# A two-layer decoder kernel: phase 2's work in a new order on all engines, and the second cross attention's scores computed as one unit

## The reference, cut to what matters

```
x = LN(x + self_attention_0(x))          16 heads, causal, with a bias      phase 1
x = LN(x + cross_attention_0(x, ctx))    16 heads, 64 keys, masked          phase 1
x = LN(x + moe_0(x))                     8 routed experts (top 2), 2 shared phase 2
x = LN(x + self_attention_1(x))          16 heads, causal, latent weights   phase 2
x = LN(x + cross_attention_1(x, ctx))    one head of 256 channels, 64 keys  phase 3
x = LN(x + ffn_1(x))                     1024 wide, sine activation         phase 3
```

```
qh = q @ Wq + bq;  kh = ctx @ Wk + bk;  vh = kh @ Wv + bv
scores = qh @ kh.T;  scores = where(mask == 0, -10000, scores)
out = softmax(scores) @ vh @ Wo + bo
```

## Time and profile before

| | value |
|---|---|
| median of 3 runs | 3624.59 us |
| profiled execution | 3628.03 us, span 3626.1 us |
| PE, PEld, DVE, ACT, POOL busy | 92%, 70%, 72%, 63%, 28% of the span |
| phase 1, with its prologue | from 0 to about 1305 us |
| phase 2 | to about 2987 us |
| phase 3 | to the end |
| mean granted TensorE clock | 0.969 of full |

### The profile page before, as it was taken

The page is one execution under the profiler, slowest core; times in us unless marked ns, Lnnn a source line. Parts: engine busy times, 40 slices in busy tenths (PEclk is TensorE's granted clock), DMA queues, the critical chain, the costliest instruction groups (busy, mean ns, idle before and its releaser), DMA issues.

```text
span 3626.1 us, 59862 instructions
## 1 busy us (share of the span) xinstructions
PE 3344.5 (92%) x20706; PEld 2528.1 (70%) x20706; DVE 2625.4 (72%) x7153; ACT 2283.5 (63%) x4067; POOL 1022.4 (28%) x1576
## 2 busy tenths in 40 slices
PE   5999999999999848999999999999999876999998
PEld 4677777777777636777777777777777655766664
DVE  5688888888888644677777777777777534788876
ACT  3677777777777622456666555556556543677776
POOL 2244444444444422222222322222223110000000
PEclk8999999999999979999999999999999877999999
DMA  7654545445544021444444444444444421011010
GB/s 193 101 95 84 88 96 107 84 88 95 107 84 82 17 82 53 84 80 77 86 92 94 94 88 88 90 89 93 92 87 88 73 44 62 12 36 35 25 35 24
DMA packets 203403, 283.27 MB, mean 78 GB/s; under 512 B 48929, under 2 KB 131874, under 8 KB 194274
## 3 DMA queue, kind: packets, MB, share of 16 engines
q1 hardware_dynamic: 203106, 279.46, 38.2%
HBM read 179.49 MB, written 96.73 MB: 76 GB/s over the span
## 4 chain that ended last, share of the span: by engine, by line
PE 71%; ACT 11%; DVE 7%; DMA 5%; issue 4%; SPq 1%; POOL 1%; PEld 0%; POOLq 0%; ACTq 0%; PEldq 0%; DVEq 0%
PE ps L829 35%; PE ps L1003 8%; PE ps L978 7%; PE ps L1201 5%; PE ps L1017 5%; ACT q_stack L1669 5%; PE ps L953 3%; DMA qk_scratch<-parts 3%; ACT pt L1686 2%; PE ps L984 1%; PE ps L1077 1%; PE ps L888 1%; PE ps L1028 1%; DMA k_stack<-qk_scratch 1%; DVE nmax L1351 1%
## 5 line engine op out<-in xcount | busy, mean ns | idle before, releaser
L1686 ACT ACTIVATE pt<-ps 128x512 f32<-128x512 f32 x1280 | 735.9, 598 | 346.7 <-PE ps L1003 338.8
L1889 POOL TENSOR_SCALAR_AFFINE_SELECT pt<-pt 128x256 f32<-128x256 f32 x1024 | 392.1, 419 | 704.9 <-ACT pt L1686 704.9
L978 PE MATMUL ps<-k_stack,q_stack 96*128 96x512 f32 (+3 forms) x2048 | 547.2, 338 | 42.3 <-ACT q_stack L1669 11.8
L1358 DVE CUSTOM_DVE_ANT_0 ps<-ps,future 128x512 f32<-128x512 f32 (+3 forms) x1024 | 481.7, 515 | 141.9 <-PE ps L978 138.8
L1003 PE MATMUL ps<-q_stack,k_stack 100*128 100x512 f32 (+3 forms) x2048 | 538.6, 345 | 29.3 <-ACT q_stack L1669 23.4
L1003 PEld LDWEIGHTS ps<-q_stack,k_stack 100*128 100x128 f32 x2048 | 351.5, 195 | 124.9 <-ACT q_stack L1669 37.2
L978 PEld LDWEIGHTS ps<-k_stack,q_stack 96*128 96x128 f32 x2048 | 355.6, 194 | 103.2 <-ACT q_stack L1669 18.8
L1351 DVE TENSOR_REDUCE nmax<-ps 128x1 f32<-128x512 f32 (+2 forms) x768 | 354.4, 502 | 92.0 <-PE ps L984 91.0
L1895 POOL TENSOR_TENSOR rs<-rs 128x4 f32<-128x4 f32 x96 | 97.1, 1012 | 1062.0 <-DVE rs L1394 1062.0
L1669 ACT ACTIVATE q_stack<-ps 4x512 fp32r<-4x512 f32 x512 | 300.8, 588 | 64.7 <-PE ps L992 56.5
L1017 PE MATMUL ps<-pt,v_ones 128*32 128x512 f32 (+3 forms) x4096 | 312.1, 446 | 5.7 <-POOL pt L1889 5.3
(11 more groups left out here) (278 smaller groups left out, 7958.6 us busy)
## 6 DMA issues: line engine op xcount, KB each, us to landing
qk_scratch<-parts SPq DMA_DIRECT2D x64, 1024.0 KB, 5.5
q_stack<-qk_scratch SPq DMA_DIRECT2D x384, 128.0 KB, 4.9
k_stack<-qk_scratch SPq DMA_DIRECT2D x384, 128.0 KB, 5.6
gate_of<-gate_scratch SPq DMA_DIRECT2D x128, 256.0 KB, 5.6
x_mid<-x_ring SPq DMA_DIRECT2D x32, 512.0 KB, 3.9
x_ring<-x_mid SPq DMA_DIRECT2D x32, 512.0 KB, 5.3
x_ring<-in_x SPq DMA_DIRECT2D x16, 512.0 KB, 3.8
out_dram<-x_ring SPq DMA_DIRECT2D x16, 512.0 KB, 2.9
```

Source lines behind the costliest of these rows:

```text
L978: done = e.matmul(bank(bank_of[piece])[:, at:at + width], a.q[0:96, base + h, t * P:(t + 1) * P], a.k[0:96, base + h, 0:width], start=a.la ...
L1358: done = e.tensor_tensor_reduce(src, src, future[:, SEQ - width:SEQ], -1.0, 3e38, ALU.add, ALU.min, nmax[:, g % 2, to:to + 1])
L1686: e.activation(dst, src, ACT.Exp).then_inc(exp_up.sem)
L1889: done = e.affine_select(out=blk, in_=blk, compare_op=ALU.is_ge, fill=0.0, base=0, pattern=[[0, 2], [1, P]], channel_multiplier=-1)
```

## The change

**Phase 2.** Every time of phase 2's table is new, on all five engines, and with it the order of the pieces and the choice of PSUM banks. No piece of phase 2 changes what it does. The table's period goes from 91.45 to 90.623. The table lines for some kinds:

```diff
-    2: (91.45, {
+    2: (90.623, {
+        "sync": {
+            "ld 2": [-78.284],
+            "send": [82.769, 104.563],
+            "rows": [112.457, 134.686, 155.546, 179.135],
+            "st 2": [279.788],
+            "gh": [-38.533],
+            "sg": [-36.173, -35.738, -26.135, -20.394, -5.291, 0.424, 9.165, 18.599],
+        },
...
         "scalar": {
-            "mr": [137.263, 139.255, 160.384, 164.751, 196.024, 196.044, 212.747, 212.767],
+            "mr": [138.106, 139.099, 158.603, 159.596, 191.074, 192.067, 210.72, 211.713],
...
         "vector": {
-            "h3": [-47.625, -31.127, -24.632, -21.3, -6.146, 7.033, 19.611, 23.072, 28.061, 40.153],
+            "h3": [-47.748, -31.792, -24.968, -18.789, -4.6, 5.128, 13.795, 20.052, 26.166, 33.951],
...
         "gpsimd": {
-            "sel": [144.512, 151.809, 165.914, 174.49, 195.45, 197.278, 214.007, 218.167],
-            "h2": [None, None, -34.818, -28.614, -14.445, -6.268, 1.14, 12.393, 18.268, 24.753],
+            "sel": [152.034, 156.648, 173.145, 180.159, 199.72, 203.91, 218.585, 226.305],
+            "h2": [None, None, -27.497, -21.756, -6.653, -2.324, 7.803, 17.237, 24.112, 31.773],
...
-        "sync": {
-            "ld 2": [-85.349],
-            "send": [76.442, 95.983],
-            "rows": [97.435, 117.928, 140.108, 160.952],
-            "st 2": [273.954],
-            "gh": [-46.706],
-            "sg": [-44.627, -44.367, -30.774, -27.299, -12.417, -5.729, 2.455, 17.582],
-        },
```

```diff
@@ phase 3's table, and pieces_of
         "gpsimd": {
+            "tb x1": [-26.6],
             "ln x1": [-4.648],
...
         put("tc", "x1", b)
+        put("tb", "x1", b)
@@ tensors
-        co_b, f2_b = sb(st3, "co_b_row", [1, DIM]), sb(st3, "f2_b_cols", [P, CT])
-        ones = sb(st3, "ones", [1, P])
+        co_b, f2_b = sb(st3, "co_b_rows", [P, DIM]), sb(st3, "f2_b_cols", [P, CT])
-        a_h, a_l = (sb(st3, f"a_{part}", [P, CT, keys_all], F32R) for part in "hl")
+        a_parts = sb(st3, "a_parts", [P, CT, BATCH, 2, CTX], F32R)
-        q_bias, seen, unseen = (sb(st3, n, [P, keys_all]) for n in ("q_bias", "seen", "unseen"))
+        seen, offset = (sb(st3, n, [P, keys_all]) for n in ("seen", "offset"))
-        LN_BIAS = {"x0": xo_b, "a1": proj_b}
+        LN_BIAS = {"x0": xo_b, "a1": proj_b, "x1": co_b}
@@ TensorE, cw
-                    ops.append((ones[:, :], co_b[:, :]))
@@ TensorE, cs
                     for t in range(TT):
                         rows = slice(t * P, (t + 1) * P)
-                        ops = []
-                        for c in range(CT):
-                            ops += three(ch[:, c, rows], cl[:, c, rows], a_h[:, c, keys], a_l[:, c, keys])
-                        done = product(e, bank(bank_of[piece])[:, t * CTX:(t + 1) * CTX], ops)
+                        both = bank(bank_of[piece])[:, 2 * t * CTX:2 * (t + 1) * CTX]
+                        done = None
+                        for c, part in ((0, ch), (0, cl), (1, cl), (1, ch)):
+                            wide = part is ch
+                            done = e.matmul(both if wide else both[:, 0:CTX], part[:, c, rows],
+                                            a_parts[:, c, b, :, :].rearrange("p a k -> p (a k)") if wide else a_parts[:, c, b, 0, :],
+                                            start=wide and c == 0, stop=wide and c == 1)
@@ VectorE, prologue of phase 3, ahead of the FFN's constants
+                        for n in range(2):
+                            cols = slice(n * 512, n * 512 + 512)
+                            e.wait_ge(bq_up, n + 1)
+                            e.wait_ge(keys_lo, 12)
+                            e.tensor_tensor(tile32[:, n, :], bank(4 + n), seen[:, cols], ALU.mult).then_inc(mine.up())
+                            e.wait_ge(*mine.now)
+                            e.tensor_tensor(offset[:, cols], offset[:, cols], tile32[:, n, :], ALU.add).then_inc(mine.up())
@@ VectorE, cs
-                    e.tensor_tensor(sc3[:, :, :], bank(bank_of[piece])[:, 0:TT * CTX].rearrange("p (t k) -> p t k", t=TT),
-                                    key_row(q_bias), ALU.add).then_inc(cs_add.sem)
+                    halves = bank(bank_of[piece]).rearrange("p (t a k) -> p t a k", t=TT, a=2)
+                    e.tensor_copy(sx3[:, :, :], halves[:, :, 1, :]).then_inc(mine.up())
+                    e.wait_ge(*mine.now)
+                    e.tensor_tensor(sc3[:, :, :], halves[:, :, 0, :], sx3[:, :, :], ALU.add).then_inc(cs_add.sem)
@@ ScalarE, prologue of phase 3
-                        for n in range(2):
-                            e.wait_ge(bq_up, n + 1)
-                            e.activation(q_bias[:, n * 512:n * 512 + 512], bank(4 + n), ACT.Copy)
@@ GpSimd
-                elif kind == "prologue":
-                    e.memset(ones[:, :], 1.0)
@@ SP
-                        e.dma_start(co_b[:, :], dram["co_b"].partition_broadcast(1)).then_inc(mask_in3, 16)
+                        e.dma_start(co_b[:, :], dram["co_b"].partition_broadcast(P)).then_inc(mask_in3, 16)
```

More of the change, by code:

```diff
@@ L210 @@
     }),
-    2: (91.45, {
-        "tensor": {
[25 rows of a table removed]
+    2: (90.623, {
[7 more added lines that the diff above has]
+        },
+        "tensor": {
[25 rows of a table added]
         },
         "scalar": {
[19 rows of a table removed]
[19 rows of a table added]
         },
         "vector": {
[18 rows of a table removed]
[18 rows of a table added]
         },
         "gpsimd": {
-            "tb a1": [63.863],
-            "sel": [144.512, 151.809, 165.914, 174.49, 195.45, 197.278, 214.007, 218.167],
-            "ln a1": [270.008],
-            "h2": [None, None, -34.818, -28.614, -14.445, -6.268, 1.14, 12.393, 18.268, 24.753],
-            "ln ex": [45.724],
-        },
-        "sync": {
-            "ld 2": [-85.349],
-            "send": [76.442, 95.983],
-            "rows": [97.435, 117.928, 140.108, 160.952],
-            "st 2": [273.954],
-            "gh": [-46.706],
-            "sg": [-44.627, -44.367, -30.774, -27.299, -12.417, -5.729, 2.455, 17.582],
+            "tb a1": [70.234],
+            "sel": [152.034, 156.648, 173.145, 180.159, 199.72, 203.91, 218.585, 226.305],
+            "ln a1": [276.346],
+            "h2": [None, None, -27.497, -21.756, -6.653, -2.324, 7.803, 17.237, 24.112, 31.773],
+            "ln ex": [54.749],
         },
@@ L761, in decoder @@
         ch, cl = sb(st3, "xh3", [P, CT, SEQ], F32R), sb(st3, "xl3", [P, CT, SEQ], F32R)
-        sc3 = sb(st3, "sc3", [P, TT, CTX])
+        sc3, sx3 = sb(st3, "sc3", [P, TT, CTX]), sb(st3, "sx3", [P, TT, CTX])
         sm3 = sb(st3, "sm3", [P, 3, TT, 1])
@@ L1156, in tensor @@
                         e.wait_ge(*free)
-                    keys = slice(b * CTX, (b + 1) * CTX)
                     for t in range(TT):
                         rows = slice(t * P, (t + 1) * P)
-                        ops = []
-                        for c in range(CT):
-                            ops += three(ch[:, c, rows], cl[:, c, rows], a_h[:, c, keys], a_l[:, c, keys])
-                        done = product(e, bank(bank_of[piece])[:, t * CTX:(t + 1) * CTX], ops)
+                        both = bank(bank_of[piece])[:, 2 * t * CTX:2 * (t + 1) * CTX]
[5 more added lines that the diff above has]
+                                            start=wide and c == 0, stop=wide and c == 1)
                     done.then_inc(cs_up.sem)
@@ L1257, in vector @@
                         e.wait_ge(*mine.now)
-                        e.tensor_scalar(unseen[:, :], seen[:, :], 10000.0, -10000.0, ALU.mult, ALU.add)
+                        e.tensor_scalar(offset[:, :], seen[:, :], 10000.0, -10000.0, ALU.mult, ALU.add)
                         e.tensor_copy(bq[:, :, :], cq_b[:, :].unsqueeze(2).broadcast_to([P, CT, P])).then_inc(circle_up)
@@ L1282, in vector @@
                                 done.then_inc(keys_lo)
-                            else:
-                                hi, lo = ((k_h3, k_l3), None, (a_h, a_l))[q // 4]
-                                e.tensor_tensor(lo[:, mt, cols], tile32[:, q % 2, :], hi[:, mt, cols].bitcast(F32),
-                                                ALU.subtract).then_inc(keys_lo)
+                            elif q // 4 == 0:
+                                e.tensor_tensor(k_l3[:, mt, cols], tile32[:, q % 2, :], k_h3[:, mt, cols].bitcast(F32),
+                                                ALU.subtract).then_inc(keys_lo)
+                            else:
+                                a_of = a_parts[:, mt, n * 8:n * 8 + 8, :, :]
+                                e.tensor_tensor(a_of[:, :, 1, :], tile32[:, q % 2, :].rearrange("p (b k) -> p b k", k=CTX),
+                                                a_of[:, :, 0, :].bitcast(F32), ALU.subtract).then_inc(keys_lo)
+                        for n in range(2):
[5 more added lines that the diff above has]
```

(13 more changed lines are left out.)

## The result

The changed kernel takes 3678.93 us (median of 4 runs, 3675.47 to 3680.09) against 3623.76 (median of 4, 3622.74 to 3631.72). The ratio is 1.0147, 95% interval 1.0133 to 1.0160. The forecast was 3563 us, the range 3538 to 3598.

The account below looks back on a forecast made before the run. TensorE was taken to bound phase 3 and nearly phase 2. Phase 2's -38 us and phase 3's -23.4 took the profiled 3628.0 to 3566.6, forecast as 3563 since that profile lies 3.4 above the median; range 3538 to 3598.

Parts of the forecast that it names:

- What becomes tight: Phase 2's shorter windows for row loads ahead of `S 1.0` and `S 2.0`: 0.9 us per period lost, bounds 0 and 2.5.
- rows 1: Phase 2's loads for `S 1.0`: a chain of 8.0 to 8.5 us against 7.5 of work, 0.5 to 1.0 late.
- 0.28 of restart: Phase 2: each TensorE stall costs 0.28 us on top of its idle time, 0.17 unreported and 0.10 of restart.
- Rival 1: Phase 2's row loads take over, costing 2.5 us per period in place of 0.9: 3585 us; chance 0.20.
- Rival 5: Slower: `rows 2` behind `sg 2` waits for a late GpSimd `h2 2`; 3628 us at 5 us of lateness; chance 0.05.
- rival 4: Phase 3 gives only about 10 us, as wide matmuls cost double or `tb x1` holds VectorE: 3577; chance 0.06.
- tb x1: Phase 3's GpSimd add, which might block VectorE passes: counted at nothing, bound 2.35 us per element.
- The four old waits: Phase 2's TensorE waits for `hid`'s low part, the maxima, the values' copy and an exp go: 3.6 us per period.
- send 0: Phase 2: issued some 8 us sooner, so ScalarE's copy ahead of the maxima at `T 2.0` no longer waits; 0.8 us goes.
- The forecast period of 92.9: Phase 2's repeating period after the change, given as a sign that the forecast is right; 95 or more would be wrong.
- The first and the last elements: Phase 2's ends, where queues run partly empty: put at 0, bounds -8 and +8 us.
- Phase 3: Fewer `cs` and `cw` matmuls -25.8 us, prologue +2.8, first element -0.4: -23.4, bounds -27 and -8.

Follow-up runs that it names:

- rows2_first: The changed kernel with `rows 2` ahead of `sg 2` in SyncE's queue, nothing else; 3608.59 us, ratio 0.9956 to the kernel before.
- gate_small: The changed kernel with `sg 2` loading its gate row to 16 partitions instead of 128, order kept (part of the gating left out); 3611.97 us.
- both_fixed: The changed kernel with `rows 2` ahead of `sg 2`, and `S 1.0` and `S 1.1` behind `tm v1`; 3596.41 us, ratio 0.9917 to the kernel before.
- s1_late: The changed kernel with `S 1.0` and `S 1.1` behind `tm v1` in TensorE's queue, nothing else; 3676.46 us, ratio 1.0131 to the kernel before.
- before_sg2: The kernel before the change with only `sg 2` moved ahead of `rows 2` in SyncE's queue; 3694.01 us, ratio 1.0193 to the kernel before.
- warm12: The changed kernel with 12 throwaway matmuls ahead of `S 2.0` in elements 1 to 14 of phase 2; 3661.84 us, ratio 1.0096.
- best2: The changed kernel with both_fixed's edits, `dn 9.0` between `S 0.3` and `S 0.4`, and `rows 0` ahead of `sg 7`; 3585.84 us, ratio 0.9886.
- p3_alone: The changed kernel with phase 2's old table, so phase 3's change alone; 3613.97 us, ratio 0.9963 to the kernel before.
- warm: The changed kernel with 22 throwaway matmuls ahead of `S 2.0` in elements 1 to 14 of phase 2; 3681.56 us, ratio 1.0158.
- best: The changed kernel with best2's edits and also `dn 0.0` ahead of `tm v1`; 3597.66 us, ratio 0.9930 to the kernel before.

## Why the prediction was wrong

**The step that failed** is the second half of "What becomes tight": "`rows 2` now stands behind `sg 2` ... an extra issue and a gate row's transfer cost 0 to 0.8". The place and the mechanism were named, the size was wrong. TensorE has 9.7 to 9.8 us of work between `T 0.9` and `S 2.0` (forecast 9.5). Before the change the six loads needed 9.0 of it, from `T 0.9` to the last landing, so 0.7 was spare. In the changed kernel they begin 0.3 later, and from the first issue to the last landing they take 12.3 in place of 9.0 (medians of ten periods; 9.0 again in rows2_first and gate_small). 0.3 + 3.4 - 0.7 = 3.0, and the wait is 3.1. So of the transfer put ahead of them all but the spare 0.7 is time of TensorE. Nothing in the forecast compared the chain of `rows 2` with that window.

For `rows 1` I did that sum, and one term of it was too small: the forecast took the median landing, 5.6, where `S 1.0` needs the last of the six, which lands 6.6 after its issue. The chain is 8.9 us, not 8.0 to 8.5, against 7.6 of work (forecast 7.5), and the wait is 1.4. (Before the change the work there was 11.1 us in the trace, not the "over 14" of the table.)

**A term that was missing:** the clock. A wait of over 3 us cost 1.71 us more in every period, where I had put 0.28 of restart on each stall, read from stalls below 1 us. With it `sg 2` costs 4.9 per period, 69 us in fourteen; the measured difference of rows2_first is 70. The 0.28 itself did not show where the experiments removed or added a wait: rows2_first fell by 4.92 for 4.89 of wait and clock, both_fixed by 1.07 for 1.03 of wait. The Trainium skill ("TensorE: Matmul & The Clock Gate", HAM oscillation — how this bites in real kernels) says that a loop that waits for a DMA in every turn starts each turn at the low clock. The trace agrees in all ten periods of the changed kernel; of the twenty such waits in s1_late and before_sg2 three had no fall behind them (waits of 2.79, 2.97 and 3.24). warm12 shows that the low clock costs time and doesn't merely stand in the records.

**Rivals.** Rival 1 (the row loads take over) is what happened, beyond its bound of 2.5 per period. Rival 5 named this very queue position, but priced it by how late GpSimd's `h2 2` might end. It ended on time; the gate row's transfer was the price, and gate_small tells the two apart. Of rival 4 the wide matmuls didn't cost double, but `tb x1` did hold VectorE, for 4 us. I gave rival 5 0.05, and 0.04 to a slower kernel. (Its sum had a slip: 5 us of lateness per period would be 3563 + 70 = 3633, not 3628.)

**Right, by steps.** The four old waits went. From the changed kernel, 98.99 less 4.58, 1.71 and 0.56 (`nmax`) is 92.14, 3.44 below 95.58. From best2, 92.67 less 0.37 (`hid`) and 0.17 (`el`) is 92.13. Both say 3.4 where the forecast said 3.6. Of it 2.5 is the idle time of the old waits; 0.9 is busy time (93.0 us per period before, 92.1 in best2), for which I had put 0.28 on each stall. Since no experiment shows that price, what made the 0.9 is open. ScalarE waits no more for `send 0`. `S 1.0` is late by 1.3 to 1.7, forecast 0.5 to 1.0. The forecast period of 92.9 is nearly that of both_fixed, 93.00, but by coincidence: the forecast had 0.9 in it for the two `rows` waits, and both_fixed has neither, but two others, 0.56 and 0.37.

**The sum, term by term:** phase 2 came to +65 us in place of -38, and some 69 of these 103 are `sg 2` ahead of `rows 2` with its low clock; phase 3 came to -12 in place of -23.4.

**Not foreseen:** `S 0.4` directly behind `S 0.3` waits 0.56 for VectorE; I had checked the old waits' places and the loads, not each pair that came to stand together.

**The first and the last elements** I put at 0, bounds -8 and +8. They cost more: against p3_alone the changed kernel loses 15.2 us before the third marker, and 8.1 behind the last one, which rows2_first gets back. To the third marker the changed kernel loses 13.7 us (1484.32 to 1498.04). In both_fixed one cause is plain: `rows 0`, now behind `sg 7`, comes 5.9 us late to the first element; with it ahead (best2) 1.9 are left. Stalls of 1.5 to 5.9 us there lower the clock, and from the first marker to the fifth (1 - clock) adds up to 15.4 us in both_fixed and 13.7 in best2 against 5.1 before. That these are worth their full time was not tried.

**Phase 3** was forecast at -23.4 and p3_alone gives 12 to 13. `cs` is as forecast: 16 matmuls in 1.74 us where 24 took 2.60, 0.86 saved (forecast 0.89). Two of 128 and two of 64 columns take 0.45 together, 0.11 on the mean, as long as four of 64 did. By the rule of the Trainium skill that the prediction cites ("TensorE: Matmul & The Clock Gate", Back-to-back issue gap) the sixteen would take 0.65; it stays contradicted:

```profile
3290.88 0.42 PE L1163 MATMUL ps<-a_parts,xh 128*128 128x128 f32 x2
3291.14 0.36 PE L1163 MATMUL ps<-a_parts,xl 128*128 128x64 f32 x2
3291.33 0.42 PE L1163 MATMUL ps<-a_parts,xh 128*128 128x128 f32 x2
```

`cw` lost 0.7 (from 3.83 to 3.14 with the pieces beside it). Of the 1.6 per period 0.4 came back: 0.27 of it before the transposes of `back`, whose weight loads wait for ScalarE (first row below); the rest is small and was not traced. The prologue's wait is 8.90 in place of 5.53, 3.4 and not 2.8 (second row, TensorE in order of time). The first two elements of phase 3 pay 4.2 more: TensorE's two waits for `x_ring`'s layer norm are 7.7 us in place of 3.5. So phase 3 gives 16 x 1.2 = 19.2, less 3.4, less 4.2: 11.6.

```profile
PEld ps L1140 <- ACT back L1801: 5.4, 10, 0.5
```

```profile
3110.69 0.58 PE L830 MATMUL ps<-w_hi,v_h 128*128 128x256 f32 x1 [8.90 <-DVEq L1334]
```

Those 4.2 are `tb x1`, which the prediction counted at nothing. In the first two elements GpSimd runs it right when VectorE has a small step of `ln x1` to do, whose inputs all lie in SBUF. That step takes 2.30 us and ends with GpSimd's add; in the kernel before it takes 0.16, and all of the layer norm behind it waits. GpSimd and VectorE in the changed kernel, then VectorE before:

```profile
3156.44 2.34 POOL L1893 TENSOR_TENSOR x_ring<-x_ring,co_b_rows 128x1024 f32<-128x1024 f32 x1
3156.49 2.30 DVE L1410 SCALAR_TENSOR_TENSOR rs<-ag,rs 128x4 f32<-128x4 f32 x1 [1.13 <-POOL rs L1907]
```

```profile
3092.77 0.16 DVE L1398 SCALAR_TENSOR_TENSOR rs<-ag,rs 128x4 f32<-128x4 f32 x1 [1.12 <-POOL rs L1895]
```

Two such steps, 2.1 us each, are the whole 4.2. (No run moved the add alone; that it is the cause rests on both steps ending with it.) In the repeating part `tb x1` holds nobody, as counted: GpSimd runs it from 3286.89, and VectorE's passes beside it read PSUM and last 0.75 each as elsewhere.

```profile
3286.89 2.44 POOL L1893 TENSOR_TENSOR x_ring<-x_ring,co_b_rows 128x1024 f32<-128x1024 f32 x1 [7.09 <-PE ps L954]
```

```profile
3287.02 1.53 DVE L1569 SCALAR_TENSOR_TENSOR ang<-tr,fc,ps 128x512 f32<-128x512 f32 x2
```

## What to carry to other kernels

When a DMA moves past another in one queue, compare the whole chain (issue, bytes ahead, landing) with the work that covers it, for every load behind the moved one. Slack that is nearly used up before the change has no room for one transfer more, however small the engine's own delay. A repeated stall of the bottleneck engine that is long enough to lower its clock costs half as much again as its idle time here (3.1 us of wait, 1.71 of clock), so such a stall is the first to remove; a smaller one removed before it may bring almost nothing, as in s1_late. Where a piece waits for several loads, it is the last landing that counts, not the median. An add moved to an idle engine should be checked in the first elements too, where the work of the others falls at other times.

## What the runs showed of the hardware

In the steady part of phase 2 the granted clock fell to 0.50 at 27 of the 30 waits of 2.6 to 3.4 us (the changed kernel, s1_late, before_sg2), at two of four waits of 1.72 to 1.85 (it fell in gate_small and warm12, and did not in gate_small's other one and in best), and behind none of 1.3 to 1.7. A fall cost 1.71 or 3.41 us of clock in the sum. A throwaway fp32 matmul of 128 columns takes 0.22 us at full clock (warm), as long as an fp32r one of 512 (0.23). A VectorE step of 4 columns with its inputs in SBUF took 2.30 us beside a GpSimd add that reads SBUF, and 0.16 without it (phase 3's first elements).
